# Uneven groups in the second expert layer: 6, 6, 2 and 2 sequences in place of 4 each, and the runs of expert blocks placed anew

## The reference, cut to what matters

```python
x = x + attn_a(layernorm(x))      # 16 heads of 8, x is 16 x 256 x 128
x = x + ffn(layernorm(x))         # first expert layer
x = x + attn_b(layernorm(x))      # selective scan, 16 states, then W_out
x = x + ffn(layernorm(x))         # second expert layer

def ffn(h):                       # 8 experts, 128 -> 512 -> 128
    logits = x @ gate_w
    top_vals, top_idx = top_k(logits, 2)
    top_w = softmax(top_vals)
    h = relu(einsum('td,edf->etf', x, w1)); out = einsum('etf,efd->etd', h, w2)
    return sum over the two chosen experts of top_w * out
```

## Time and profile before

| what | value |
|---|---|
| median of 3 runs | 1487.36 us (1479.74 to 1489.97) |
| the profiled execution | 1482.02 us, span of its instructions 1480.3 us |
| PE, DVE, ACT, POOL busy, share of the span | 68%, 56%, 50%, 43% |
| mean granted TensorE clock | 0.788 of 2.4 GHz |
| DMA, mean rate over the span | 102 GB/s |

### The profile page before, as it was taken

The page is one execution under the profiler, slowest core; times in us unless marked ns, Lnnn a source line. Parts: engine busy times, 40 slices in busy tenths (PEclk is TensorE's granted clock), DMA queues, the critical chain, the costliest instruction groups (busy, mean ns, idle before and its releaser), DMA issues.

```text
span 1480.3 us, 18066 instructions
## 1 busy us (share of the span) xinstructions
PE 1006.6 (68%) x5080; PEld 742.0 (50%) x5080; DVE 827.8 (56%) x2789; ACT 745.5 (50%) x2034; POOL 633.3 (43%) x672
## 2 busy tenths in 40 slices
PE   4778588757787755588697863678688647871371
PEld 2555377625666433457476622366476316650371
DVE  3677655655565775655566673745656754662111
ACT  4777676646555755545566652352454443450020
POOL 2100400173342537560424268785455686456304
PEclk8565589858797857788888956789889867995696
DMA  9000424222322011334434221254444223523472
GB/s 267 4 1 0 127 93 148 79 85 88 103 88 84 13 33 58 121 96 138 132 105 139 79 81 32 84 160 157 128 150 164 84 63 118 160 83 101 129 220 73
DMA packets 101812, 150.65 MB, mean 102 GB/s; under 512 B 9840, under 2 KB 72688, under 8 KB 101584
## 3 DMA queue, kind: packets, MB, share of 16 engines
q1 hardware_dynamic: 88832, 129.20, 27.9%
q0 software_dynamic: 8528, 18.19, 4.3%
q10 hardware_dynamic: 4352, 2.10, 0.5%
HBM read 125.39 MB, written 28.25 MB: 104 GB/s over the span
## 4 chain that ended last, share of the span: by engine, by line
PE 36%; DVE 20%; ACT 16%; POOL 12%; issue 10%; DMA 4%; another core or an unknown queue 2%; SPq 1%; POOLq 0%; DVEq 0%; ACTq 0%
PE eo_bank L1300 9%; PE h_bank L1285 8%; ACT sc_bank L644 7%; PE sc_bank L1234 6%; DVE Pw L892 4%; POOL xg L564 3%; POOL rings L508 3%; DVE rings L902 3%; DVE nmx L836 3%; PE mix_bank L1157 2%; PE sc_bank L1178 2%; POOL gbuf L577 2%; ACT rings L689 2%; DVE eos L1024 2%
## 5 line engine op out<-in xcount | busy, mean ns | idle before, releaser
L1300 PE MATMUL eo_bank<-wring,hid 128*128 128x128 f32 x1472 | 222.0, 300 | 84.9 <-DVE eos L1024 81.5
L644 ACT ACTIVATE sc_bank<-sc_bank,nmx 128x256 f32<-128x256 f32 x512 | 229.8, 457 | 45.7 <-DVE nmx L836 41.4
L1300 PEld LDWEIGHTS eo_bank<-wring,hid 128*128 128x128 f32 x1472 | 202.5, 213 | 96.2 <-ACT hid L718 51.7
L1285 PE MATMUL h_bank<-xT,wring 128*128 128x128 f32 x1472 | 226.6, 302 | 34.6 <-DVE xT L1012 22.0
L1285 PEld LDWEIGHTS h_bank<-xT,wring 128*128 128x128 f32 x1472 | 204.7, 212 | 70.5 <-issue 33.7
L718 ACT ACTIVATE hid<-h_bank 128x512 f32<-128x512 f32 x184 | 109.2, 594 | 230.2 <-PE h_bank L1285 215.3
L508 POOL TENSOR_TENSOR rings<-Rs,Abc 128x512 f32<-128x512 f32 x128 | 163.0, 1288 | 138.9 <-ACT Rs L672 83.1
L1234 PE MATMUL sc_bank<-Pw,upto 128*128 128x512 f32 x256 | 165.7, 747 | 57.9 <-DVE Pw L892 57.2
L836 DVE TENSOR_REDUCE nmx<-sc_bank 128x2 f32<-128x512 f32 x256 | 169.8, 684 | 58.1 <-PE sc_bank L1178 47.5
L577 POOL DMA_INDIRECT gbuf<-yg,pos x128 | 122.9, 960 | 168.2 <-issue 102.0
L902 DVE SCALAR_TENSOR_TENSOR rings<-sc_bank,bc,rings 128x128 f32<-128x128 f32 x512 | 143.0, 342 | 74.5 <-PE sc_bank L1234 74.2
(11 more groups left out here) (155 smaller groups left out, 1364.5 us busy)
## 6 DMA issues: line engine op xcount, KB each, us to landing
wring<-wcat SPq DMA_DIRECT2D x184, 512.0 KB
stage<-xg SPq DMA_DIRECT2D x40, 256.0 KB, 5.0
yg<-eos SPq DMA_DIRECT2D x40, 256.0 KB
wcat<-in_w SPq DMA_DIRECT2D x16, 256.0 KB, 5.2
X<-in_x SPq DMA_DIRECT2D x16, 128.0 KB, 5.1
xg<-xnb,pos POOLq DMA_INDIRECT x128
gbuf<-yg,pos POOLq DMA_INDIRECT x128
out<-X ACTq DMA_DIRECT2D x16, 128.0 KB
```

Source lines behind the costliest of these rows:

```text
L644: last = act.activation(sc[r % NSC][:, c * L:(c + 1) * L], sc[r % NSC][:, c * L:(c + 1) * L], ACT.Exp, bias=nmx[:, c, r:r + 1], accum_out= ...
L1285: last = pe.matmul(hb[b % 2][:, f], wring[:, n % WR, 0, f], xT[:, b % 2], start=True, stop=True)
L1300: last = pe.matmul(eo[:, o:o + P], hid[:, b % 2, f], wring[:, n % WR, 1, f], start=(k == 0), stop=(k == FC - 1))
```

## The change

The groups of layer 2 get 6, 6, 2 and 2 sequences; layer 1 keeps four times 4. The blocks of a run become 31, 31, 15 and 15 in layer 2 (92 as before), its slots 24, 24, 8 and 8. Sizes (slots_of, blocks_of, NBS, STORES, FIRST) are now per run, and the semaphore values that were products of one size are counted by functions (block_at, rows_scattered, stage_loads, stores_done, all_stored; class Runs replaces Progress for the runs' three semaphores). eb, pos and tw get a place for every group in place of one or two, so the wait ahead of the write of eb goes; two seg constants more; iotab, le and cnt go from 24 to 31 entries. In a phase with a front, two slots are scattered after each exponent product in place of one. The runs start at other places and are spread anew; the gathers of layer 2 too; the phases become 36.

```diff
-    GS = 4
-    NSLOT = GT * K
-    NB = (NSLOT * P - E) // P + E
+    GROUPS = {1: (4, 4, 4, 4), 2: (6, 6, 2, 2)}
+    def slots_of(ly, g):
+
+        return GROUPS[ly][g] * T * K
+
+    def blocks_of(ly, g):
+
+        return (slots_of(ly, g) * P - E) // P + E
...
-            eb[ly] = sb(f"eb{ly}", [P, 24], I32)
+            eb[ly] = sb(f"eb{ly}", [P, len(GROUPS[ly]), NB], I32)
...
-        RUN_FIRST = {(1, 0): (6, 1, 40), (1, 1): (10, 1, 60), (1, 2): (17, 1, 46), (2, 0): (20, 1, 46), (1, 3): (25, 1, 30),
-                     (2, 1): (27, 1, 30), (2, 2): (30, 1, 30), (2, 3): (34, 0, 25)}
+        RUN_FIRST = {(1, 0): (6, 1, 40), (1, 1): (10, 1, 60), (1, 2): (17, 1, 60), (2, 0): (22, 1, 46), (1, 3): (25, 1, 30),
+                     (2, 1): (30, 1, 31), (2, 2): (32, 1, 16), (2, 3): (34, 0, 17)}
...
-        for g, n in enumerate(([23, 24, 25, 26], [29, 30, 31, 31], [32, 33, 33, 33], [36, 36, 36, 36])):
-            for q in range(GS):
-                final.setdefault(n[q], []).append(GS * g + q)
-        PHASES = 37
+        for b, n in enumerate((26, 27, 28, 29, 30, 31, 32, 33, 33, 33, 33, 33, 35, 35, 35, 35)):
+            final.setdefault(n, []).append(b)
+        PHASES = 36
...
                 if j == 0 and g >= 2:
-                    sp.wait_ge(*comb_dve[ly].at("x", GS * (g - 2) + GS - 1))
+                    sp.wait_ge(*comb_dve[ly].at("x", sum(GROUPS[ly][:g - 1]) - 1))
...
                 for n in range(2):
-                    pool.wait_ge(s_yg[n], 16 * (STORES // 2) * (r + 1))
+                    pool.wait_ge(s_yg[n], all_stored(r, n))
...
                     for k in chunks:
                         scan_exponents(front[n], k)
-                        scatter_rows(n, 8 + k, 9 + k)
+                        scatter_rows(n, 8 + 2 * k, 10 + 2 * k)
...
-                if g:
-                    dve.wait_ge(*run_pe.at(f"dn{NB - 1}", RUNS.index((ly, g - 1))))
-                dve.tensor_scalar(eb[ly][:], cnt[:], float(E - 1), None, ALU.min).then_inc(*ro.done("eb"))
+                dve.tensor_scalar(eb[ly][:, g], cnt[:], float(E - 1), None, ALU.min).then_inc(*ro.done("eb"))
```

More of the change, by code:

```diff
@@ L241, in moe_hybrid_kernel @@
         s_scat = sem("rows_scattered")
-        s_xg = [sem(f"stage_loaded{n}") for n in range(STORES)]
+        s_xg = [sem(f"stage_loaded{n}") for n in range(max(STORES))]
         s_yg = [sem(f"rows_stored{n}") for n in range(2)]
@@ new lines, in moe_hybrid_kernel, with block_at @@
+        run_act = Runs(sem("run_act"), [[f"h{b}" for b in range(n)] for n in NBS])
+        run_dve = Runs(sem("run_dve"), [["xT0"] + [e for b in range(n) for e in ([f"xT{b + 1}"] if b + 1 < n else [])
+                                                   + ([f"eo{(b - 2) // 4}"] if b % 4 == 1 and b > 4 else [])] + [f"eo{s - 1}"]
+                                        for n, s in zip(NBS, STORES)])
+        def block_at(n):
+            r = max(r for r in range(len(RUNS)) if FIRST[r] <= n)
+            return r, n - FIRST[r]
@@ new lines, in rows_scattered, with stage_loads, stores_done, all_stored @@
+        def rows_scattered(r):
+            return 16 * sum(NSLOTS[:r + 1])
+        def stage_loads(r, j):
+            return 16 * sum(1 for s in STORES[:r + 1] if j < s)
+        def stores_done(r, j):
+            return 16 * (sum(len(range(j % 2, s, 2)) for s in STORES[:r]) + j // 2 + 1)
+        def all_stored(r, parity):
+            return 16 * sum(len(range(parity, s, 2)) for s in STORES[:r + 1])
+        RUN_FIRST = {(1, 0): (6, 1, 40), (1, 1): (10, 1, 60), (1, 2): (17, 1, 60), (2, 0): (22, 1, 46), (1, 3): (25, 1, 30),
+                     (2, 1): (30, 1, 31), (2, 2): (32, 1, 16), (2, 3): (34, 0, 17)}
@@ L347, in run_events @@
                 k = (n - p) * HALVES + half - h
-                events += [(r, e) for e in range(NB + 2) if e * (halves - 1) // (NB + 1) == k]
+                events += [(r, e) for e in range(NBS[r] + 2) if e * (halves - 1) // (NBS[r] + 1) == k]
             return events
         def scatter_of(n):
-            return [(ly, b // GS) for ly, at in ((1, tail_a), (2, tail_s)) for b in [at.get(n - 1)] if b is not None and b % GS == GS - 1]
+            return [(ly, group_of[ly][b][0]) for ly, at in ((1, tail_a), (2, tail_s)) for b in [at.get(n - 1)]
+                    if b is not None and last_of_group(ly, b)]
         def mp_free_after(ly, b):
-            return (route_dve[ly], "a2", b // GS) if b % GS == GS - 1 else (prep_dve[ly], "topi", b)
+            return (route_dve[ly], "a2", group_of[ly][b][0]) if last_of_group(ly, b) else (prep_dve[ly], "topi", b)
         def has(b):
@@ L445, in _ @@
                     load_block_weights(r, b)
-                for j in range(STORES):
+                for j in range(STORES[r]):
                     load_stage(r, j)
-                for b in range(WR, NB):
+                for b in range(WR, NBS[r]):
                     load_block_weights(r, b)
@@ L451, in _ @@
                         store_rows(r, (b - 7) // 4)
-                for j in range((NB - 8) // 4 + 1, STORES):
+                for j in range((NBS[r] - 8) // 4 + 1, STORES[r]):
                     store_rows(r, j)
@@ L555, in scatter_rows @@
                     r = RUNS.index((ly, g))
+                    if last is None:
+                        last = NSLOTS[r]
                     if first == 0:
```

270 lines of the change are left out of this document (148 added, 122 removed).

## The result

The change makes the kernel 1.4% slower: 1511.16 us (median of 4 runs, 1501.21 to 1515.0) against 1488.66 us for the kernel before on the same chip (4 runs, 1479.74 to 1499.13). The ratio is 1.0138, with a 95% interval of 1.0072 to 1.0203. The profiled execution took 1501.21 us against 1482.02.

A forecast was written before the change was run, and what follows sets the result against it. No single engine bounds the kernel (PE has 36% of the waits); place matters. Terms -31.4 + 23.2 + 11.8 + 12.3 - 20.1 - 22.9 + 19.6 sum to -7.5 us; forecast 1479.5 us, range 1456 to 1498.

The forecast's parts named there:

- (a): End of the kernel: 8 blocks fewer in the last run, 8 gathers instead of 16 behind it; -31.4 us.
- (b): Phase 31 half 8 to the last group's first scatter: more blocks beside the last scan's tail; +23.2 us.
- (c): Phases 29 and 21: 24 scatters in one phase, two after each product, lengthen POOL's queue; +11.8 and +12.3 us.
- (d): Phases 16 to 21 and 25 to 29, which scatters or blocks leave, get shorter; -20.1 and -22.9 us.
- (e): Phases 22 to 25 and 30, where blocks come: +9, +9, -2.4 and +4, together +19.6 us.
- rival 4: At the end, sequence 14's wait or the buffers hold back the early gathers; +10 us, time 1490, chance 0.10.
- PE's idle time stays about 43: Before the last run: POOL's count of scatters and gathers stays 28, so PE idles about 43 us as before.
- rival 2: Emptied phases 27, 28 and 21 give nothing back, as PE falls to 1.2 GHz; at most +23 us, chance 0.12.
- my even price per block: Covered expert blocks in any stretch: each costs 0.87 us in single phases, about 0.9 in the paired region.
- Rival 1: Dense phases 22 to 24 and 30 to 32: PE bounds, 25 blocks cost their bare 2.68 us; +45, chance 0.18.
- (f): Constants, wider eb, pos and tw, and new waits throughout cost nothing: 0 us, constants bounded by -1 and +3.
- Rival 3: POOL not the bound, run joins free: (c) costs 8, (b) 14; sum -32 us, time 1455, chance 0.15.

The follow-up runs named there:

- f0: The changed kernel, unchanged, run again on a faster chip beside its variants: 1478.99 us, 1.0065 of the kernel before.
- e1: The changed kernel's code with the old groups of 4, old places of the runs, old gathers and single scatters: 1467.32 us, 0.9986 of the kernel before.
- h1: The changed kernel with run (2, 2) started at half 4 of phase 32 in place of half 1: 1503.94 us, 1.0103 of the kernel before.
- e3: The changed kernel with run (2, 2) moved to phase 33 and that phase's five adds spread over its halves: 1467.58 us, 0.9995 of the kernel before.
- f2: The changed kernel with (2, 2) from half 8 of phase 32 over 24 halves, phase 33's adds spread: 1466.20 us, 0.9986 of the kernel before.
- f3: e1 with eight more scatters in phase 29, one after each product, to an unread DRAM buffer: 1480.32 us, 1.0072 of the kernel before.
- e2: e1 with (1, 2) over 60 halves, (2, 0) from phase 22 and gathers of sequences 0 to 8 later: 1455.10 us, 0.9898 of the kernel before.
- h3: e2 run again, unchanged, on a slower chip: 1487.81 us, 0.9984 of the kernel before.
- g4: e1 with gathers and adds of sequences 9 to 11 moved to phase 34: 1475.91 us, 0.9883 of the kernel before; repeated on another chip, 0.9939.
- e4: The changed kernel with the paired scatters moved behind all exponent products and the scan's adds: 1500.98 us, 1.0204 of the kernel before.

## Why the prediction was wrong

The forecast was -7.5 us on the profile; it became +19.2. The mechanisms named were there, but four terms were mis-sized: the tail's halves, the wait of the last run, the first blocks of (2, 1) and the price of a block in a stretch that is already full. The chip added to it, so the split is given twice, for the first profile against the kernel before, and for f0 against e1 on the two faster chips:

| part | forecast | first profile | f0 against e1 |
|---|---|---|---|
| (a) end | -31.4 | -25.6 | -27.5 |
| (b) tail | +23.2 | +30.9 | +28.0 |
| (c) phases 21 and 29 | +24.1 | +30.9 | +25.8 |
| (d) phases that give | -43.0 | -44.6 | -44.2 |
| (e) phases that take | +19.6 | +28.6 | +27.8 |
| ahead of phase 16 | 0 | -0.9 | -3.0 |
| sum | -7.5 | +19.2 | +6.8 |

The last column is some us too low in its sum, since e1's profiled execution (1473.88 us) is 6.6 us above the median of e1's runs.

(a) The end. The last run fell by 20.8 us (forecast 21.4), the part behind it by 9.1 (10.0): rival 4, no early gathers, is out. But the step "PE's idle time stays about 43" failed: first scatter to first transpose grew by 4.3, and by 2.1 in f0 against e1. The last copy of (2, 2) and, behind it, the adds of sequences 7 and 8 come late, and POOL's gather waits for them (the end, above). In f0 the same copy waits 2.88 us in place of 10.44 (last section). h1 shows POOL's wait at 12.18 us. In all -25.6, forecast -31.4.

(b) The tail was mis-sized: +30.9, forecast +23.2. Its parts: last mark to the end of the dense phase's halves 1317.66 to 1344.51, 26.9 us (25.6); to the first transpose at 1356.50 12.0 (11.3); to the first scatter 37.9 (32.2). The third one failed: a half with one block and the tail's own work costs 37.9 / 12 = 3.16 us, not 2.68, the price of a block with nothing beside it. e3 and f2 show the cause: with (2, 2) out of the way the stretch is 49.7 and 51.9. Counted by their transposes, 35 blocks (5 of (2, 1), 15 and 15) start behind the last mark, where before there were 26 (3 + 23). A block moved from the last run to the tail stays exposed: (a) and (b) together are +5.3, and the 8 blocks saved at the end were paid in front of it.

(c) Phase 29: +19.1 (f0 against e1 +16.0), forecast +11.8. Order of time of the changed kernel there, POOL and PE:

```profile
1186.29 1.27 POOL L571 TENSOR_TENSOR rings<-Rs,Abc 128x512 f32<-128x512 f32 x1
...
1190.03 1.27 POOL L571 TENSOR_TENSOR rings<-Rs,Abc 128x512 f32<-128x512 f32 x1
...
1216.33 1.27 POOL L583 TENSOR_TENSOR ysum<-rings 128x512 f32<-128x512 f32 x1
...
1220.47 0.47 PE L1346 MATMUL h_bank<-ident,stage 128*128 128x128 f32 x1 [9.59 <-DMA stage<-xg]
1225.78 2.07 PE L1355 MATMUL h_bank<-xT,wring 128*128 128x128 f32 x8 [4.83 <-DVE xT L1084]
...
1227.86 1.80 PE L1303 MATMUL sc_bank<-Pw,upto 128*128 128x512 f32 x2
```

and of the kernel before, PE:

```profile
1218.22 0.48 PE L1276 MATMUL h_bank<-ident,stage 128*128 128x128 f32 x1 [5.97 <-DMA stage<-xg]
1218.49 1.91 PE L1234 MATMUL sc_bank<-Pw,upto 128*128 128x512 f32 x2
```

The products stand 3.74 us apart, as forecast (3.75), and the 8 scatters cost 8.8 us by f3 (forecast 10.1). The later start of (2, 1) is in those 8.8 us already: PE waits 9.59 us for its stage here, 8.18 in f3 and 4.31 in e1. What I left out comes behind that wait. 31 blocks over 31 halves put two events into the first half, so the first block's passes up stand ahead of the scan's last sums and wait for DVE's copy (4.83 us); the sums begin 7.4 us behind the first transpose, before 0.3. Between f0 (72.0) and f3 (64.8) lie 7.2 us, two blocks are 1.7 of it; that this order is the other 5.5 is argued, no run takes it away alone. In the first profile 3.1 us more come with the slower chip. Phase 21: +11.8, forecast +12.3, right in the sum and by luck: e2 with 3 blocks and no scatter takes 32.9 us, e1 with 7 blocks 43.0, f0 with 3 blocks and the scatters 52.9. So four blocks fewer gave 10.1, not 4.4, and the 16 scatters behind the mark cost 20.0, where I had 16.7 for all 24. The stretch 618.50, which I had read as one with 16 scatters, has 8 of them, and the stretch ahead of it the other 8; in phase 29 it is 12 and 4.

(d) Phases 16 to 21 gave back 20.1 (forecast 20.1), by luck, since two misses cancel: up to half 5 of phase 20 it was 22.6 in place of 13.5, and phase 20 to 21 gave +2.5 in place of -6.6. Part of both is work that I had left where it was: the first group's routing and its first 8 scatters moved from the stretch 16 to 17 (POOL 28 instructions, now 20) to 20 to 21 (7, now 14); with them goes the difference of 4.2 us between f0 (42.0) and e2 (37.8) there. The other part is what rival 2 forecast for an emptied phase, nothing given back: on one chip e1's 10 blocks at clock 1.00 take 36.7 us and e2, emptied, 37.8 at 0.61. Its reason, the clock, is not shown (31.1 us at 0.51 in the stretch 14 to 15). Phases 25 to 29 gave 24.5 (22.9), with 41.0 us for the stretch without blocks, so rival 2 is out there, though the clock was at 0.71. The rule of the Trainium skill that I weighed ("TensorE: Matmul & The Clock Gate", section "HAM oscillation — how this bites in real kernels") agrees with the granted clocks, 0.61 and 0.71 in the emptied stretches; what the clock cost in phase 20 is not separated, and in phase 27 it took nothing from the gain.

(e) Phase 22 to 23 grew by 18.5, forecast +9; 23 to 24 by 9.8 (+9); 24 to 25 by -2.6 (-2.4); 30 to 31 by 2.9 (+4). The first one is +8.7 in f0 against e1 (45.2 against 36.5), but my even price per block was wrong. e2 has 10 blocks in that stretch and takes 36.7, no more than e1 with 3; the four from there to 14 cost 8.5 us, 2.1 each. In 30 to 31 f0 takes 64.6 us and e1 56.6 with four blocks fewer, 2.0 each. So seven blocks were nearly free, and those on top of a full stretch (PE busy 31.6 of 36.7 us in e2) came near the bare 2.68. Rival 1 is not out: the 25 blocks cost 31.2 us (18.5 + 9.8 + 2.9), 30.2 in f0 against e1, where I had 22. That is 0.33 to 0.37 us a block above my price, just over the 0.3 at which I had called it decisive, and far below the 1.8 at which I had priced it whole. On the slower chips the stretch 22 to 23 is longer still, 52.6 to 59.2 us in the changed kernel and its variants and 44.7 in h3, e2's program.

(f) 0 by e1.

The misses add up: the stretches up to the last mark are 13.2 off (+13.9 for +0.7), of which (c) is 6.8, (e) 9.0 and (d) -1.6, and about -1 lies ahead of phase 16; what lies behind it is 13.5 off, 7.7 in (b) and 5.8 in (a). Rival 3 (POOL not the bound, run joins free) is out by f3 and by the 10.59 and 9.59 us at the two joins. No rival had the outcome alone: it was the forecast's own steps, each a few us dearer, with a small share of rival 1, and a spread of 12 us around it that was too narrow for terms of 20 to 30 us that nearly cancel.

## What to carry to other kernels

A shorter last group moves work in front of the last scatters; it pays only if that place has cover. Count the blocks behind the last covered phase before and after (26 and 35 here) and not only those of the last run. Look at what stands between the first and the last scatter of the last group: taking the gathers of three sequences out of it (g4) was worth 0.6 to 1.2% without any regrouping, while the uneven groups cost 1.3 to 1.7% on top of e2. A price per block that is an average over a stretch does not hold for the next block: here it was nearly nothing from 3 to 10 and 2.1 us from 10 to 14. And where a forecast is a sum of large terms of both signs, the range must come from their sizes, not from the small sum.

## What the runs showed that I had not expected

The same program differs by chip in more than a scale: the kernel before took 1467.8, 1468.8, 1489.5 and 1487.8 us on the four. In the profiles of the two faster chips the waits name no idle time from an unknown releaser (remote); in those of the slower they do, as in the changed kernel's first profile (waiting engine, releaser, total us, times, longest):

```profile
ACT hid L784 <- remote: 12.1, 3, 5.5
DVE eos L1093 <- remote: 10.4, 1, 10.4
DVE xT L1084 <- remote: 8.6, 4, 4.1
```

In all this kind of idle time was 36.3 us in the kernel before, 44.7 after, 43.1 in h3 and none in e2, which is the same program as h3 and 32 us shorter in span (1454.0 and 1486.1). In spite of its name this is TensorE. In the traces of the kernel before, the changed kernel and h3 the semaphore that ended each of these waits is one that TensorE alone counts up, 1.6 to 6.6 us behind the end that the records give its matmuls, which is modelled. For the copy at 1410.00 the last passes down end at 1403.33 by the records, and their signal came at 1409.98. So on these chips TensorE at times finished later than its records say; why, no run shows. A gain of 1% measured on one chip was gone on the other, so a difference of this size should be measured on more than one chip.

An indirect scatter on POOL between the scan's products cost the stretch 1.1 us (8.8 / 8, f3). Behind the products and adds scatters were not cheaper: there (e4) the changed kernel had 1.0204, between them (f0) 1.0065, on two chips on which the kernel before is within 1 us of itself.
